# Basis matrices of a graph layer in chunks of 120 rows instead of 128, in a ring of five loads

## The reference

```python
w = jnp.einsum('rb,bio->rio', att, basis)      # r: 2 relations, b: 30 bases, i, o: 512
x_j = x[col]
for r in range(2):
    gate = jax.nn.sigmoid(x_j @ gate_w[r, :, 0])
    msgs.append(gate[:, None] * x_j @ w[r])
msg = jnp.where((edge_type == 0)[:, None], msgs[0], msgs[1])
agg = jax.ops.segment_sum(msg, row, num_segments=x.shape[0])
return agg + x @ root + bias
```

## Time and profile before

| | us |
|---|---|
| median of 3 runs | 1014.03 |
| fastest, slowest | 1012.87, 1028.96 |
| the profiled execution: span, first to last instruction | 1014.3 |
| TensorE busy in it | 945.3 (93%) |
| VectorE | 556.8 (55%) |
| ScalarE | 400.6 (39%) |
| HBM read in it | 120.40 MB |

### The profile page before, as it was taken

One profiled execution on the slowest core, in us unless ns is written; L12 is line 12 of the kernel. 1 busy time (PEld: TensorE's weight loads), 2 busy tenths in 40 slices (PEclk: granted clock), 3 DMA queues, 4 the chain that ended last, 5 costly groups with the idle time before them and its releaser, 6 DMA issues. The chain is left out here.

```text
span 1014.3 us, 12428 instructions
## 1 busy us (share of the span) xinstructions
PE 945.3 (93%) x4724; PEld 612.8 (60%) x4724; DVE 556.8 (55%) x1176; ACT 400.6 (39%) x670; POOL 109.6 (11%) x98
## 2 busy tenths in 40 slices
PE   3789889799999999999999899989999899999998
PEld 1245445257454476458775655889998644445885
DVE  5588887742227541334212772498777643558871
ACT  3467775331111211111111332468786553423550
POOL 0000000000020023100002000144331000022300
PEclk9899999799999999998999999999999999999899
DMA  8888988852000102016595400513101300230001
GB/s 305 281 341 332 336 325 343 321 196 90 0 14 6 51 3 83 1 46 233 199 319 187 172 0 1 172 43 84 43 1 44 123 1 3 87 83 0 1 2 50
DMA packets 53039, 124.87 MB, mean 123 GB/s; under 512 B 5408, under 2 KB 19492, under 8 KB 52963
## 3 DMA queue, kind: packets, MB, share of 16 engines
q1 hardware_dynamic: 51314, 121.46, 33.9%
q0 software_dynamic: 1120, 1.29, 0.5%
q10 hardware_dynamic: 528, 1.05, 0.3%
HBM read 120.40 MB, written 3.38 MB: 122 GB/s over the span
## 5 line engine op out<-in xcount | busy, mean ns | idle before, releaser
L409 PE MATMUL PS<-AR 128*125 128x512 f32 (+9 forms) x1394 | 394.0, 440 | 9.0 <-issue 1.9
L409 PEld LDWEIGHTS PS<-AR 128*128 128x128 f32 (+3 forms) x1394 | 212.5, 194 | 169.0 <-issue 161.9
L442 PE MATMUL PS<-AR 128*32 128x512 f32 x576 | 88.2, 628 | 35.4 <-DMA AR<-in_basis 34.4
L1949 ACT ACTIVATE AR<-PS 128x500 f32<-128x500 f32 (+6 forms) x73 | 41.9, 578 | 167.3 <-PE PS L409 81.5
L1952 ACT ACTIVATE AR<-iota,AR 125x625 f16<-125x625 f16 x119 | 86.1, 810 | 39.1 <-PE PS L495 38.9
L442 PEld LDWEIGHTS PS<-AR 128*32 128x32 f32 x576 | 19.4, 111 | 91.0 <-issue 56.2
L1278 DVE TENSOR_SCALAR AR<-iota,AR 125x625 f16<-125x625 f16 x165 | 60.5, 442 | 17.6 <-PE PS L495 17.6
L493 PE MATMUL PS<-AR 125*125 125x512 f16 (+9 forms) x425 | 61.2, 302 | 3.5 <-issue 3.4
L493 PEld LDWEIGHTS PS<-AR 125*125 125x125 f16 x425 | 46.2, 142 | 21.7 <-issue 12.3
L2447 POOL TENSOR_TENSOR whl<-AR,whh 128x512 fp32r<-128x512 f32 x32 | 47.8, 1513 | 89.8 <-ACT whh L1949 89.8
L1797 DVE TENSOR_TENSOR HMl<-AR,HMh 128x626 fp32r<-128x626 f32 x64 | 51.3, 841 | 4.6 <-ACT HMh L1949 4.6
(11 more groups left out here) (318 smaller groups left out, 1479.1 us busy)
## 6 DMA issues: line engine op xcount, KB each, us to landing
AR<-in_basis SPq DMA_DIRECT2D x80, 768.0 KB, 8.3
AR<-in_L_ffn_W SPq DMA_DIRECT2D x20, 1024.0 KB, 7.8
AR<-in_L_gnn_Wh SPq DMA_DIRECT2D x8, 512.0 KB, 4.0
AR<-in_L_gnn_Wh SPq DMA_DIRECT2D x16, 256.0 KB, 4.7
AR<-in_L_mix_W_qkv SPq DMA_DIRECT2D x1, 3072.0 KB, 11.3
AR<-in_L_gnn_root SPq DMA_DIRECT2D x2, 1024.0 KB, 14.7
y_dram<-AR SPq DMA_DIRECT2D x8, 256.0 KB, 8.1
AR<-in_WkvT SPq DMA_DIRECT2D x1, 2048.0 KB, 8.6
```

Of the source, the lines that this page charges most:

```text
L409: ins = te.matmul(o, l, r, start=start and i == 0, stop=stop and i == len(pairs) - 1)
L442: ins = te.matmul(CB[32 * j:32 * j + 32, :], Am[:, l, m, 16 * (n % 2):16 * (n % 2) + 32], ring[:, at // 3, at % 3, :], start=m == quarter[ ...
L1949: return se.activation(o, i, ACT.Copy, scale=scale)
```

## The change

The chunks get 120 rows, which are 4 input rows x 30 bases, so that four chunks are exactly one quarter (480 rows). A load holds one chunk of every quarter: 120 rows of 4 x 512 floats (8 KB), 960 KB. An n needs four loads and 16 matmuls, four after each load, one on each quarter; after the fourth of them the slot is free. There are 64 loads. `Am` needs only four blocks of 48 columns for a layer instead of 18, as all quarters share them, and VectorE makes it with `tensor_scalar` on 120 partitions. The ring still has five slots: four in the room of the old ring and the 2 KB of a partition behind it (5 x 6 KB before, 4 x 8 KB now), the fifth in a tensor of its own, `ring4`; 12 KB of a partition come from `dynamic_dma_scratch_size`, the room for GpSimd's DMA descriptors, which is set to 4,096 bytes from its default of 16,384. `combos(14)` and `combos(15)` are cut at other places, and the bias loads follow load 32 instead of 40.

```diff
--- before.py
+++ after.py
@@ -30,10 +30,9 @@
 
 
 
-PARTS = ((0, 0), (4, 1), (8, 2), (12, 3), (1, 0), (5, 1), (9, 2), (13, 3), (2, 0), (6, 1), (10, 2), (14, 3),
-         (3, 0), (3, 1), (11, 2), (11, 3), (7, 1), (7, 2))
-ORDER = (0, 4, 8, 12, 1, 5, 9, 13, 2, 6, 10, 14, 3, 11, 7)
-FREES = (2, 5, 8, 11, 17)
+ROWS = 120
+LOADS = 64
+SLOTS = 5
 
 AFTER = [g // 2 + 2 if g % 2 else None for g in range(NS)]
 FLUSHES = (NS + PER - 1) // PER
@@ -176,6 +175,7 @@
         y_dram = nc.dram_tensor("y_dram", (1025, 512), F32, kind="Internal").ap()
         arena = (nc.sbuf_base + 63) // 64 * 64
         sb("slab", [128, 48320 + 16])
+        ring4 = sb("ring4", [128, 4, 512])
         AR = nc.alloc_sbuf_tensor_at("AR", [128, 48320], F32, offset=arena)
 
         def fr(name, off, *dims, p=128):
@@ -230,9 +230,9 @@
         W = [ar(oW1, 2, 4, 512), ar(oW2, 2, 4, 512)]
 
 
-        Am = ar(oA, 2, 18, 48)
-        amask, att = ar(oW2, 18, 16), ar(oW2 + 512, 18, 2, 2)
-        ring = ar(oR2, 5, 3, 512)
+        Am = ar(oA, 2, 4, 48, p=ROWS)
+        amask, att = ar(oW2, 4, 16, p=ROWS), ar(oW2 + 512, 2, 2, p=ROWS)
+        ring = [ar(oR2 + 2048 * i, 4, 512, p=ROWS) for i in range(4)] + [ring4[0:ROWS, :, :]]
         ei = ar(oOT, 3, EP).bitcast(I32)
         ef = ar(oB + 1024, 3, EP, p=P)
         ge_ = ar(oOT + 512, NT + 1, EP, p=P)
@@ -432,17 +432,16 @@
                 ins.then_inc(u.sem, 1)
 
 
-            def combos(n, a=0, b=len(PARTS)):
+            def combos(n, a=0, b=4):
                 l = n // 8
                 pe.wait_ge(w_ready, n)
-                for m, (c, j) in list(enumerate(PARTS))[a:b]:
-                    at = ORDER.index(c)
-                    pe.wait_ge(d_ring[at // 3], 16 * (n + 1))
-                    quarter = [k for k, part in enumerate(PARTS) if part[1] == j]
-                    ins = te.matmul(CB[32 * j:32 * j + 32, :], Am[:, l, m, 16 * (n % 2):16 * (n % 2) + 32],
-                                    ring[:, at // 3, at % 3, :], start=m == quarter[0], stop=m == quarter[-1])
-                    if m in FREES:
-                        ins.then_inc(combo_done, 1)
+                for j in range(a, b):
+                    m = 4 * n + j
+                    pe.wait_ge(d_ring[m % SLOTS], 16 * (m // SLOTS + 1))
+                    for q in range(4):
+                        ins = te.matmul(CB[32 * q:32 * q + 32, :], Am[:, l, j, 16 * (n % 2):16 * (n % 2) + 32],
+                                        ring[m % SLOTS][:, q, :], start=j == 0, stop=j == 3)
+                    ins.then_inc(combo_done, 1)
 
             psum.held.add(3)
             pe.wait_ge(am_ready, 6)
@@ -510,22 +509,22 @@
 
             psum.free = [[(flush_done, NT * FLUSHES)] for _ in range(3)] + [[(flush_done, NT * FLUSHES), (w_ready, 16)]]
             psum.held.update((0, 1))
-            combos(14, 0, 6)
+            combos(14, 0, 1)
             pe.wait_ge(d_r1e, 16)
             for s, v in psum.free[0]:
                 pe.wait_ge(s, v)
             root1(0, bank[0])
-            combos(14, 6, 12)
+            combos(14, 1, 3)
             root1(1, bank[1])
-            combos(14, 12)
+            combos(14, 3)
             u = psum.take("many", "dve", slot=2)
             slot(u)
             pe.wait_ge(many_ready, 1)
             te.matmul(sl(u.slot, 0, 10, 1), ones[0:P, 0:1], sm[0:P, 3, 0:2, 0:5], start=True, stop=True).then_inc(u.sem, 1)
             root1(2, bank[2])
-            combos(15, 0, 6)
+            combos(15, 0, 2)
             root1(3, bank[3])
-            combos(15, 6)
+            combos(15, 2)
             psum.held.discard(3)
 
 
@@ -1222,8 +1221,7 @@
             dv.wait_ge(d_att, 32)
             for lay in range(2):
                 for k in range(3):
-                    ve.tensor_tensor(Am[:, lay, :, 16 * k:16 * k + 16], amask,
-                                     att[:, :, lay, k % 2].unsqueeze(2).to_broadcast([128, 18, 16]),
+                    ve.tensor_scalar(Am[:, lay, :, 16 * k:16 * k + 16], amask, att[:, lay, k % 2:k % 2 + 1], None,
                                      ALU.mult).then_inc(am_ready, 1)
             dv.wait_ge(d_edge, 16)
             ve.tensor_scalar(nsrc, ei[0:P, 0, :], -STEEP, STEEP / 2, ALU.mult, ALU.add).then_inc(nsrc_ready, 1)
@@ -1284,7 +1282,7 @@
             def combo_in(k):
 
                 l, kc = k // 8, k % 8 // 2
-                dv.wait_ge(combo_done, 5 * (k + 1))
+                dv.wait_ge(combo_done, 4 * (k + 1))
                 dv.wait_ge(w_ready, k)
                 for r in range(2):
                     ins = ve.scalar_tensor_tensor(out=W[l][:, r, kc, :], in0=CB, scalar=halves[1 - r], in1=W[l][:, r, kc, :],
@@ -1984,7 +1982,7 @@
 
                 l, kc = k // 8, k % 8 // 2
                 ac.wait_ge(d_cst, 16)
-                ac.wait_ge(combo_done, 5 * (k + 1))
+                ac.wait_ge(combo_done, 4 * (k + 1))
                 for r in range(2):
                     ins = copy(W[l][:, r, kc, :], CB, scale=halves[r])
                 ins.then_inc(w_ready, 1)
@@ -2479,26 +2477,26 @@
             ye.dma_start(iota[:, :], A["c_iota"]).then_inc(d_iota, 16)
 
             def load_basis(n):
-                r = n % 5
-                if n > 4:
-                    sp.wait_ge(combo_done, n - 4)
-                ye.dma_start(ring[:, r, :, :], A["basis"][n]).then_inc(d_ring[r], 16)
+                r = n % SLOTS
+                if n >= SLOTS:
+                    sp.wait_ge(combo_done, n - SLOTS + 1)
+                ye.dma_start(ring[r], A["basis"][n]).then_inc(d_ring[r], 16)
 
             ye.dma_start(X[:, :, :], A["x"].rearrange("c p f -> p c f")).then_inc(d_x, 16)
             ye.dma_start(cst[:, :], A["c_cst"]).then_inc(d_cst, 16)
-            for n in range(5):
+            for n in range(SLOTS):
                 load_basis(n)
             def load_gates(lay, d):
                 ye.dma_start(gw[lay][0:P, :, :].rearrange("p r i -> p (r i)"), A["gate_w"][lay:lay + 1, :].to_broadcast([P, 1024])).then_inc(d, 16)
 
             load_gates(0, d_gw0)
-            for n in range(5, 80):
+            for n in range(SLOTS, LOADS):
                 load_basis(n)
-                if n == 40:
+                if n == 32:
                     sp.wait_ge(gl_ready, NT)
                     ye.dma_start(bias1, A["bias1"]).then_inc(d_bias, 16)
                     ye.dma_start(bias2, row(A["L0_gnn_bias2"]).to_broadcast([P, 512])).then_inc(d_bias2, 16)
-            sp.wait_ge(combo_done, 80)
+            sp.wait_ge(combo_done, LOADS)
             ye.dma_start(Wqkv, kp(A["L0_mix_W_qkv"])).then_inc(d_wqkv, 16)
             ye.dma_start(R1, kp(A["L0_gnn_root1"])).then_inc(d_r1, 16)
             ye.dma_start(R2, kp(A["L0_gnn_root2"])).then_inc(d_r2, 16)
@@ -2624,10 +2622,10 @@
     group = (128 * np.arange(4)[:, None, None, None] + 16 * np.arange(2)[:, None, None] + 32 * np.arange(4)[:, None]
              + np.arange(16)).reshape(8, 64)
     a["basis"] = np.stack([g["L0_gnn_basis1"], g["L0_gnn_basis2"]])[:, :, group].transpose(0, 2, 3, 1, 4).reshape(
-        16, 15, 128, 512)[:, list(ORDER)].reshape(80, 3, 128, 512).transpose(0, 2, 1, 3)
-    flat = 128 * np.array([c for c, _ in PARTS])[None, :] + np.arange(128)[:, None]
-    a["att"] = np.stack([g["L0_gnn_att1"], g["L0_gnn_att2"]])[:, :, flat % 30].transpose(2, 3, 0, 1)
-    a["c_amask"] = (flat[:, :, None] // 30 == np.arange(16) + 16 * np.array([j for _, j in PARTS])[:, None]).astype(np.float32)
+        16, 4, 4, ROWS, 512).transpose(0, 2, 3, 1, 4).reshape(LOADS, ROWS, 4, 512)
+    rows = np.arange(ROWS)
+    a["att"] = np.stack([g["L0_gnn_att1"], g["L0_gnn_att2"]])[:, :, rows % 30].transpose(2, 0, 1)
+    a["c_amask"] = (4 * np.arange(4)[:, None] + rows[:, None, None] // 30 == np.arange(16)).astype(np.float32)
     a["gate_w"] = np.stack([g["L0_gnn_gate_w1"], g["L0_gnn_gate_w2"]]).reshape(2, 1024)
     a["fb1"] = g["L0_ffn_b1"].reshape(8, 4, 128).transpose(2, 0, 1)
     a["bh1"] = g["L1_gnn_bh1"].reshape(16, 4, 128).transpose(2, 0, 1)
@@ -2649,7 +2647,7 @@
         np.tile(np.tile(128 * np.arange(1, 5, dtype=np.float32), 8), (128, 1)),
         np.tile((1 + 1024 * np.arange(8, dtype=np.float32)[:, None] + 128 * np.arange(1, 5)).reshape(32), (128, 1)),
         np.arange(128)[:, None] // 16 % 2 == np.arange(2)], axis=1).astype(np.float32)
-    nc = bacc.Bacc("TRN2", target_bir_lowering=False, num_devices=1)
+    nc = bacc.Bacc("TRN2", target_bir_lowering=False, num_devices=1, dynamic_dma_scratch_size=4096)
     arrays, args = {}, {}
     for name, v in a.items():
         v = np.ascontiguousarray(v)
```

## The result

| | before | after |
|---|---|---|
| median of 4 runs | 1013.45 | 1086.66 |
| fastest, slowest | 1008.54, 1028.96 | 1083.88, 1091.63 |
| ratio, 95% interval | | 1.0754 (1.0701 to 1.0807) |
| profiled execution: span | 1014.3 | 1082.1 |
| first z product | 218.8 | 287.1 |

The ratio is of fast runs alone, without the one of 1028.96, and is not the quotient of the two medians.

The account below looks back on a forecast made before the run. It took TensorE, VectorE and the DMA engines as all near their limit in the stage's middle. Head 0, middle -9 and tail -1 gave -10 us from 1014.3: 1004 us, own range 995 to 1011, 992 to 1062 with the slow case.

Parts of the forecast that it names:

- Loads: Basis loads: 120 rows go over 15 engines at the 128-row pace, 2.5 us a load, 10.0 for an n's four.
- the rival: Basis loads: the fifteen engines get in each other's way; 1058 us, up to 1133; chance 0.26.
- The point from which it decides: Load time at which four loads take longer than the present 11.8 us cycle: 2.95 us a load.
- Matmuls: Bursts: four rounds instead of five, 4.49 to 3.63 us each, 13.8 us in all, not all on the path.
- Ring: Five slots for four loads an n let loads run ahead; nearly all 12.4 us of late loads go.
- Middle: Stage from burst 2 to 13: plain cycles fall from 11.0 to about 10.1 us, together -9 us.
- Head: Stage until burst 1 ends at 41.6 us: +0.5 for loads and matmuls, -0.5 for an earlier stream, 0 us.
- Tail: Stage from 177.5 us to the z products at 218.8: root weights +1.5, burst pieces -2.5, together -1 us.
- -2.5 for the pieces: Tail, 192.2 to 218.8 us: pieces of bursts 14 and 15 need seven rounds instead of nine, -2.5 us.
- +1.5 for the root weights: Tail: root weights share engines with larger basis packets, so their 14.6 us load grows, +1.5 us.
- Scratch: Smaller descriptor scratch: GpSimd's five gathers, landing 5.8 us after issue, cost nothing more.
- No gain: Rival: the DMA share stays 0.87, the middle gains 6 us and root weights and head take most back; 1011 to 1018; chance 0.14.

Follow-up runs that it names:

- m1_rows: Kernel of loads alone, eight per shape, in different row counts: eight loads of 128 rows took 22.2 us, eight of 120 rows 39.6.
- m2_steps: Loads alone, mainly the same 11 rows on different partitions: 7.8 us when 12 apart, 12.8 when 8 apart, 20.7 on neighbouring partitions.
- e3: Kernel before the change, with only 120 of each chunk's 128 rows loaded and multiplied: 1086.05 us (one run).
- e1: Changed kernel with each load padded by eight rows of zeros to 128 rows, still 120 in each matmul: 1010.94 us, ratio 0.9974 to the kernel before.
- e2: e1 with the gate weights also broadcast to 128 partitions instead of 125: 1004.8 us, ratio 0.9918 to the kernel before.
- e4: e2 with a ring of four slots, without `ring4`, and with the default descriptor scratch: 1011.86 us, ratio 1.0005 to the kernel before.
- e5: Kernel before the change, with only the gate weights broadcast to 128 partitions instead of 125: 1005.42 us, ratio 0.9946.
- e6: e2 with two bias rows also broadcast to 128 partitions and each 125-row store cut into 112 and 13: 998.59 us, ratio 0.9875 to the kernel before.

## Why the prediction was wrong

**The step that failed is *Loads*:** "2.33 x 16/15 = 2.5 us". Its count was right: 15 engines, a share of 0.95. What it took over from the 128-row loads unseen was each engine's pace, and 1.86 us for 768 KB holds only when every engine has a way of its own. A load took 3.9 to 4.1 us. "120 rows in eights are then on each engine what 128 are on 16" is true of the number of rows and false of their places. m1_rows shows the slow loads without the kernel and m2_steps that the partitions decide it; e3 has nothing but the 120 rows in the old kernel and is as slow, and e1 takes them away and gets the 2.5.

**The row that could have told** was in the prediction: 224 GB/s at a share of 1.02. It was read rightly, as every engine at 0.52 of its pace, and the right rival was made of it. Then it was played down, because a 125-row load alone had full pace. That argument does not hold: m1_rows has the same (133 GB/s at 0.32), and 120 rows alone at half pace beside it. Five engines with 25 rows each are a different pattern from fifteen with eight; the lone load said nothing about fifteen. The port map of the Trainium skill, cited there (SBUF — State Buffer, "Door 1: The DMA port swizzle"), spoke for the rival too, and e2 fits it (418 to 427 GB/s once the row goes to 128 partitions). The same section's rule, that the rate goes by the ports reached, read alone would not have: 120 partitions are on all sixteen.

**The rival's price was too low, its sum near.** It had 3.6 us a load for half conflict and 4.8 for full. With the 4.0 measured, its own sum gives 64 x 4.0 + 11.7 + 9.3 + 10 = 287.0 for the z products; they begin at 287.1. That it comes out to 0.1 us is luck. In the trace the gate load costs 7.4 us more, not 9.3; the last load lands at 282.9, 4.2 before the z products, not 10; and two pauses that the sum doesn't have, 4.7 us before load 33, which was issued behind the bias loads, and 4.7 in loads 55 to 58, while the root weights were under way, make up for it. The point from which it decides, 2.95 us a load, was passed by a third. What it did not name, the clock (0.81 for 0.97), is inside the measured 42.8 us of the middle, but hardly lengthens the stage by itself, as far as the rows tell: the DMA share is 0.95 over the whole window, fifteen engines full, so the loads set the pace, and TensorE's slower matmuls fill what would have been waits. No run tried it.

**Matmuls: the burst is right.** A burst at full speed takes 3.64 us in e1 and e4 (forecast 3.63, before 4.49). In the change itself it buys nothing, since the loads decide; what the four rounds buy by themselves no run shows, and e4 beside e5 leaves little room for it.

**Ring: right in kind.** e4 against e2 gives it 9 us; the prediction had put 12.4 us of late loads on it, less what VectorE and the DMA's 10.0 us give back.

**Middle:** +42.8 where -9 was forecast; in e1, with the loads at the pace that the forecast assumed, -8.4. A cycle there is 121.8/11 = 11.1 us, VectorE busy 106 of 121.8. In e2 it is -5.3, at a granted clock of 0.93. (In the prediction "8 x 0.9 = 7.4" is 7.2; the 7.4 is 88.2 - 8 x 10.1.)

**Head:** +16.5 to burst 2 for 0. In e1 it is +3.4. In e2 it is -6.3, and the gate edit alone gives -6.9 (e5). So the gate load, which I costed in the rival alone, is a term of the head in every case, through the wait in burst 1 and the clock behind it.

**Tail:** +9.0 for -1; in e1 -1.5. The -2.5 for the pieces was right: from the first root product to the z products it takes 24.2 us, where it took 26.6. What was mis-sized is the +1.5 for the root weights: they took 25.9 us from issue to landing (236.89 to 262.81), where they took 14.5, while the basis loads beside them ran at half pace. In e1 they take 16.8.

**Scratch: right.** The gathers' row after, beside the earlier trace rows:

```profile
L2429 POOL DMA_INDIRECT AR<-y_dram,gidx x5: 1210/1214/1386, 611.8 to 618.0; - x5
...
DMA to landing us min/median/max: 5.8/5.8/5.8
```

They land in 5.8 us each, as before (5.4 to 6.0), and nothing behind the stage is longer.

**With that one term put right the forecast would still have been too low.** In e1 the middle and the tail come out within 1 us of it and the head does not; at the z products e1 is 6.5 us ahead of the kernel before, and e2 6.7 ahead of e5, where -10 was forecast. The runs say less still: 0.26% and 0.28%, some 3 us. The profiled executions of the kernel before and of e5 took longer than most of theirs (span 1014.3 against a median span of 1010.8; 1009.12 us against a median of 1005.42), those of e1 and e2 were not, so the 6.5 and 6.7 flatter the change by some 3.5. In its time, 1010.94 us, e1 is the rival *No gain* (1011 to 1018), which had 0.14.

The chance of 0.26 was too small for a rate that had been seen halved in the very stretch where this stage begins.

**What stays open.** How deep the conflict is: 120-row loads alone have packets of 580 ns (m1_rows) and 651 ns (m2_steps), in the change 526. Engines that share a way seem to fall in and out of step, but no run shows that. Nor does one show why nearly all of the eleven engines were slow 8 apart, or what but the stores' 1.7 us makes e6's step over e2: 0.4% by the ratios, within their intervals.

## What to carry to other kernels

Count a DMA's rows before trimming them: a load of 128 rows of which 8 are thrown away was 1.6 times as fast as the same load without them (2.5 against 3.9 to 4.1 us). Read the DMA's share and its rate together, as their quotient is the engine's pace; here a share near 1 at half the rate was engines in each other's way, and a single small load of another row count (one gate row, 0.5% of the kernel) did it to the loads beside it. Compare an edit with the kernel that has every other edit too: e2 looks like 0.8% for the change, of which 0.5% are the gate row's. And when a row of the profile already shows a mechanism, the burden lies on the reason why it should not return, not on the rival.

## What the runs showed of the hardware that was not expected

- Loads of 120, 112, 96 and 64 rows move 211, 261, 257 and 210 GB/s, one of 128 rows 412 to 424, although 112, 96 and 64 rows keep 16 engines busy. 128 is not just the best of them: it is the only one of these counts at full pace.
- A load of 125 rows uses five engines at full pace when alone (133 GB/s at 0.32), and in the kernel the rate of all sixteen was halved while one ran beside the basis (224 GB/s at 1.02). In m2_steps a 125-row load of the same 4 KB rows beside 128-row loads took it down less (325 GB/s over 27 us).
- TensorE's granted clock was 0.50 and 0.56 in the stretches behind waits of 6.7 and 4.2 us, and before it was 0.50 from 32.3 to 37 us, behind one of 5.46, and 1.00 again from 41.6; in e1 it was back only in the window that starts at 51 us. In e2, where the loads are there at burst 1, burst 2 begins 9.7 us earlier than in e1; how much of that is the wait and how much the clock wasn't tried.
